# Second layer: VectorE's passes for statistics, quantisation and feed-forward at other quads of a batch

## The reference

```python
x = x + _L0_attn_ref(_layernorm(x), ...)      # layer 0: causal attention, 16 heads of 8
x = x + _L0_ffn_ref(_layernorm(x), ...)       # layer 0: 8 experts, 2 per token
x = x + _L1_attn_ref(_layernorm(x), ...)      # layer 1: full attention, 16 heads of 8
x = x + _L1_ffn_ref(_layernorm(x), ...)       # layer 1: gated, width 352

def fp4_quant_dequant(x):                     # blocks of 16 along the last axis
    scale = max(max|block| / 6, 1e-12)
    q = nearest of (0, .5, 1, 1.5, 2, 3, 4, 6) to |x / scale|
    return q * sign(x) * scale
gate, y = fp4_linear(x, w_gate), fp4_linear(x, w_up)
h = silu(gate) * y
return fp4_linear(h, w_down)                  # h is quantised too
```

## Time and profile before

| | us |
|---|---|
| median of three runs | 2297.63 (2297.55 to 2308.24) |
| profiled execution, its own time | 2295.53 |
| its span from first to last instruction | 2293.8 |
| TensorE busy | 1985.7 (87%) |
| VectorE busy | 1588.6 (69%) |
| ScalarE busy | 1396.3 (61%) |
| GpSimd busy | 1078.2 (47%) |

### The profile page before, as it was taken

The page is one execution under the profiler, slowest core; times in us unless marked ns, Lnnn a source line. Parts: engine busy times, 40 slices in busy tenths (PEclk is TensorE's granted clock), DMA queues, the critical chain, the costliest instruction groups (busy, mean ns, idle before and its releaser), DMA issues.

```text
span 2293.8 us, 45190 instructions
## 1 busy us (share of the span) xinstructions
PE 1985.7 (87%) x13603; PEld 994.7 (43%) x13603; DVE 1588.6 (69%) x4202; ACT 1396.3 (61%) x3097; POOL 1078.2 (47%) x1777
## 2 busy tenths in 40 slices
PE   2999999999999939999828889999999999899984
PEld 1455455554455419989701223333333333333333
DVE  3888888887888633332126788888888887888844
ACT  0466666666666624444305677777777777777772
POOL 6433746547455250000064565666656665664222
PEclk7899999999999969999957999999999999999997
DMA  6232223223232024444312222222222122221100
GB/s 176 79 96 68 86 75 89 76 73 92 69 92 78 24 67 144 142 136 139 108 57 72 65 62 61 65 62 61 61 65 69 57 60 65 62 61 49 54 6 14
DMA packets 167648, 174.15 MB, mean 76 GB/s; under 512 B 42544, under 2 KB 126192, under 8 KB 167280
## 3 DMA queue, kind: packets, MB, share of 16 engines
q1 hardware_dynamic: 157776, 153.87, 22.7%
q0 software_dynamic: 8192, 16.79, 2.6%
q10 hardware_dynamic: 1440, 0.60, 0.1%
HBM read 120.30 MB, written 49.28 MB: 74 GB/s over the span
## 4 chain that ended last, share of the span: by engine, by line
PE 23%; DVE 15%; issue 5%; SPq 3%; ACT 2%; POOL 2%; DMA 1%; ACTq 0%; DVEq 0%; POOLq 0%
DVE l_rowmax L1818 8%; PE bank L1604 6%; PE bank L1592 5%; PE pair L1581 3%; SPq L78 2%; PE bank L1678 2%; PE bank L1651 2%; PE pair L1658 2%; DVE l_hq L236 2%; PE bank L1618 1%; DVE l_stats L1854 1%; DVE l_hq L259 1%; POOL l_chosen_rows L1404 1%; SPq L98 1%; PE bank L1668 1%
## 5 line engine op out<-in xcount | busy, mean ns | idle before, releaser
L1818 DVE TENSOR_REDUCE l_rowmax<-pair 128x2 f32<-128x1024 f32 x512 | 597.0, 1216 | 145.7 <-PE pair L1581 145.5
L1727 ACT ACTIVATE l_probs<-bank 128x512 f32<-128x512 f32 x1024 | 554.1, 602 | 95.4 <-PE bank L1592 90.1
L907 DVE CUSTOM_DVE_ANT_0 pair<-pair,mask_rows_q 128x512 f32<-128x512 f32 (+3 forms) x1024 | 476.0, 517 | 98.3 <-PE pair L667 91.7
L823 ACT ACTIVATE l_probs<-bank 128x256 f32<-128x256 f32 (+3 forms) x769 | 307.6, 444 | 107.8 <-PE bank L679 104.6
L1592 PE MATMUL bank<-q_stack,k_stack 128*128 128x512 bf16 x1024 | 321.0, 389 | 26.2 <-DMA q_stack<-l_rowmaxT 13.6
L667 PE MATMUL pair<-k_stack,q_stack 96*128 96x512 bf16 (+3 forms) x1024 | 315.2, 313 | 25.2 <-DVE l_rowmax L907 14.9
L1604 PE MATMUL bank<-l_probs,v_aug 128*32 128x512 f32 x2048 | 276.7, 612 | 2.6 <-ACT l_oT L1772 2.6
L1581 PE MATMUL pair<-k_stack,q_stack 64*128 64x512 bf16 x1024 | 177.6, 394 | 93.3 <-DVE l_rowmax L1818 63.6
L677 PE MATMUL bank<-q_stack,k_stack 128*128 128x256 bf16 (+3 forms) x769 | 231.8, 306 | 0.2
L691 PE MATMUL bank<-l_probs,v_aug 128*32 128x512 f32 (+3 forms) x2048 | 192.2, 448 | 20.3 <-ACT l_probs L823 17.7
L1592 PEld LDWEIGHTS bank<-q_stack,k_stack 128*128 128x128 bf16 x1024 | 74.9, 97 | 253.0 <-ACT l_probs L1727 135.1
(11 more groups left out here) (286 smaller groups left out, 3383.2 us busy)
## 6 DMA issues: line engine op xcount, KB each, us to landing
q_stack<-scratch SPq DMA_DIRECT2D x192, 96.0 KB
k_stack<-scratch SPq DMA_DIRECT2D x192, 96.0 KB
experts_w<-in_w SPq DMA_DIRECT2D x72, 256.0 KB, 2.5
q_stack<-scratch SPq DMA_DIRECT2D x320, 48.0 KB
k_stack<-scratch SPq DMA_DIRECT2D x320, 48.0 KB
scratch<-l_q_parts SPq DMA_DIRECT2D x32, 384.0 KB, 2.5
scratch<-l_k_parts SPq DMA_DIRECT2D x32, 384.0 KB, 2.6
experts_rows<-rows_in SPq DMA_DIRECT2D x72, 128.0 KB, 2.2
```

Source lines behind the costliest of these rows:

```text
L823: nc.scalar.activation(probs[:, (a * HG + j) % PSLOTS, c0:S], bank[:, c0:S], ACT.Exp, scale=SCALE).then_inc(t_read, 1)
L907: nc.vector.tensor_tensor_reduce(scores, scores, m["mask_rows_q"][:, S - keys(t):S], 1.0, LOWEST, ALU.add, ALU.max, rowmax[:, g % 2, c:c + ...
L1727: nc.scalar.activation(probs[:, (a * HG + j) % PSLOTS, :], bank[:, :], ACT.Exp, scale=SCALE).then_inc(t_read, 1)
L1818: nc.vector.tensor_reduce(largest, banks[:, :].rearrange("p (k n) -> p k n", k=2), X_AXIS, ALU.max).then_inc(s_read, 1)
```

## The change

Only the tables of offsets in `layer_one` change, and with them the first and the last slot. `stats` moves from position 12 to 7, `stats4` from 0 to 15, the two `up` from one slot (position 11) into two (10 and 11) with all four `gate` in the first of them, `hquotient` from 13 to 14, `hraised` from 15 to 1, `hlowered` from 0 to 2. What depends on them moves along: `gather`, `combine` and `factors` by five slots earlier, `turn` and both `down` by one slot later.

```diff
     MIDDLE = [("rowmax", g, 4 * g + 6) for g in range(G)] + [
-        ("xnT", 0, -15), ("xqT", 0, F + 32)] + [("turn", k, F + 44) for k in range(NC)]
-    END = [("out", g, F + 4 * g + 6) for g in range(G)] + [("v", 0, 0), ("qk", 0, -9), ("qk", 1, -8)] + [("gate", t, F + 33) for t in range(2)] + [("up", 0, F + 33)] + [
-        ("gate", t, F + 33) for t in range(2, TT)] + [("up", 1, F + 33), ("down", 0, F + 45), ("down", 1, F + 53)]
-    ACT_WORK = [("normalise4", 0, F + 24), ("xsizes", 0, F + 27), ("hsizes", 0, F + 36)]
-    DVE_WORK = [("stats", 0, -20), ("stats4", 0, F + 22), ("xlargest", 0, F + 25), ("xquotient", 0, F + 26),
-                ("xraised", 0, F + 28), ("xlowered", 0, F + 29), ("hinverse", 0, F + 34), ("hquotient", 0, F + 35),
-                ("hraised", 0, F + 37), ("hlowered", 0, F + 38)]
+        ("xnT", 0, -15), ("xqT", 0, F + 31)] + [("turn", k, F + 45) for k in range(NC)]
+    END = [("out", g, F + 4 * g + 6) for g in range(G)] + [("v", 0, 0), ("qk", 0, -9), ("qk", 1, -8)]
+    END += [("gate", 0, F + 32), ("gate", 1, F + 32), ("up", 0, F + 32), ("gate", 2, F + 32), ("gate", 3, F + 32), ("up", 1, F + 33), ("down", 0, F + 46), ("down", 1, F + 54)]
+    ACT_WORK = [("normalise4", 0, F + 23), ("xsizes", 0, F + 26), ("hsizes", 0, F + 37)]
+    DVE_WORK = [("stats", 0, -25), ("stats4", 0, F + 21), ("xlargest", 0, F + 24), ("xquotient", 0, F + 25),
+                ("xraised", 0, F + 27), ("xlowered", 0, F + 28), ("hinverse", 0, F + 35), ("hquotient", 0, F + 36),
+                ("hraised", 0, F + 39), ("hlowered", 0, F + 40)]
     POOL_WORK = [("split_max", g, 4 * g + 5) for g in range(G)]
-    POOL_WORK += [("gather", k, -30 + (0, 1, 3, 4)[k // 2]) for k in range(2 * TT)]
-    POOL_WORK += [("combine", 0, -22), ("combine", 1, -21), ("factors", 0, -19), ("normalise", 0, -17),
-                  ("split", 0, -8), ("split", 1, -7), ("add_x", 0, F + 21), ("factors4", 0, F + 23),
-                  ("xscales", 0, F + 26), ("xq", 0, F + 30), ("hscales", 0, F + 34), ("hq", 0, F + 39), ("add_down", 0, F + 55)]
+    POOL_WORK += [("gather", k, -35 + (0, 1, 3, 4)[k // 2]) for k in range(2 * TT)]
+    POOL_WORK += [("combine", 0, -27), ("combine", 1, -26), ("factors", 0, -24), ("normalise", 0, -17),
+                  ("split", 0, -8), ("split", 1, -7), ("add_x", 0, F + 20), ("factors4", 0, F + 22),
+                  ("xscales", 0, F + 25), ("xq", 0, F + 29), ("hscales", 0, F + 35), ("hq", 0, F + 41), ("add_down", 0, F + 56)]
     SP_WORK = [("max_out", g, 4 * g + 7) for g in range(G)] + [("parts", 0, -6), ("parts", 1, -5)]
-    SP_WORK += [("stack", g, (-4, -2, 1, 5)[g]) for g in range(G)] + [("store", 0, F + 56)]
-    FIRST, LAST = -30, QUADS * NB + F + 41
+    SP_WORK += [("stack", g, (-4, -2, 1, 5)[g]) for g in range(G)] + [("store", 0, F + 57)]
+    FIRST, LAST = -35, QUADS * NB + F + 42
```

## The result

| | before | after |
|---|---|---|
| median of the runs, same chip | 2297.59 (2292.82 to 2308.24, 4 runs) | 2330.1 (2319.8 to 2332.07, 4 runs) |
| profiled execution, its own time | 2295.53 | 2331.56 |
| its span | 2293.8 | 2329.8 |
| first row of the layer (GpSimd's copy of the slots, L1402) | 1139.23 | 1145.21 |
| from there to the first scores | 52.73 | 64.24 |

The changed kernel is slower: ratio 1.0126, with a 95% interval from 1.008 to 1.0172. The two profiled spans differ by 36.0 us. The other 30.0 are the layer's.

A forecast was written before the change was run, and what follows sets the result against it. VectorE and TensorE take turns as the bound, so a batch costs the longer one's work per quad. Start 10.4, batches 5.6 and end 1 sum to 17 us: 2312.5 profiled, 2314.6 as median, range 2296 to 2336.

The forecast's parts named there:

- The spreading itself brings nothing: Steady batch: sum falls at positions 12, 13, 15 and rises at 1, 2, 8, 10; plus 0.5 us a batch.
- the longer list: Per position, the longer of VectorE's and TensorE's own work; sums to 63.6 us a batch before, 64.1 after.
- the fourth rival: Spreading works: TensorE's wait for VectorE falls from 4.0 to 1.0 us a batch, 42 saved, 2267 in total; chance 0.08.
- The stall behind the table load: Position 11: TensorE stands 1.2 us for ScalarE's exponential, the later last up no longer covering the load; plus 1.0 a batch.
- the drain rival: ScalarE's table switch: an uncovered drain as long as the load, 1.28 us, and the collision staying; 30 more, 2344; chance 0.08.
- Position 11: Place of the table load's standstill of 1.2 us, forecast to rise from VectorE's 3.99 to 5.0.
- the 0.8 a batch: Handovers the plain sum lacks: of 1.1 us a batch, 0.8 kept because the stall behind normalise4 falls under position 2.
- `hquotient`'s collision goes: Position 14: GpSimd's normalise ends before hquotient starts, taking 0.84 us off each batch; bounds 0.84 and nothing.
- The first rival: Collision stays: GpSimd is 0.9 late, hquotient keeps its 2.45 us; 14 x 0.84 = 12 more, 2326; chance 0.12.
- The start: GpSimd's queue before quad 0: batch 1's combine and factors precede batch 0's split, first scores 10.4 us later; bounds 10 and 12.
- the third rival: The start is paid back: quad slack absorbs the table stall and more, 0.7 to 0.8 us a batch; 2298; chance 0.22.
- The end: Last batch: stats4 moves earlier while hlowered and what follows fall later; plus 1 us, between -3 and +2.

The follow-up runs named there:

- e7: Kernel before with only turn, down, hq, add_down, store and the passes on h at their new offsets: 2302.28 us (1 run), batch 65.5 to 66.5.
- e4: Kernel before with stats, gather, combine and factors five slots earlier for batches 2 and up: 2290.44 us (1 run), batch 64.28.
- e8: Kernel before with stats, gather, combine and factors five slots earlier from batch 2, hlowered one slot later: 2277.57 us (4 runs), ratio 0.9915.
- e5: Changed kernel with a plain copy of the gate in place of silu, so no table switch: 2316.49 us (1 run), batch 65.92.
- e6: Kernel before with a plain copy of the gate in place of silu, so no table switch: 2291.3 us (1 run), batch 64.69.
- e3: Changed kernel with add_down, and store with it, two slots later on GpSimd: 2317.18 us (1 run), batch 65.65.
- e10: Changed kernel with normalise five slots earlier and add_down eight later: 2353.31 us (1 run, kernel before 2360.93 there), batch 65.27.
- e1: Changed kernel with batches 0 and 1 keeping the old offsets of gather, combine, factors and stats: 2322.88 us (1 run).
- the reordered one: Kernel before with stats and GpSimd's entries moved from batch 2, hlowered one slot later: 2311.33 us, ratio 0.9788; again 2325.73 us, ratio 0.9811.
- e11: Kernel before, unchanged, run again in a group where its median was 2371.4 us: 2372.59 us (1 run), batch 66.3 to 69.5.

## Why the prediction came out right, and what in it was wrong

Forecast was 2314.6 within 2296 to 2336, and slower at 0.62; measured 2330.1. The direction and most of the mechanisms held, but a steady batch grew by 1.53, four times the 0.4 that I gave it and more than my upper bound of 1.3. That the batches together stayed under the +18 of that bound is luck: only seven of the 13 intervals grew by the full 1.5. Held against the account above, the sum of 17 was 2.2 short at the start, 10.1 short in the batches (15.7 for 5.6) and 0.8 short at the end; with them it makes the layer's 30.

- **The spreading itself brings nothing** (+0.5 a batch): the positions agree where neither a collision nor the split `up` reaches (0, 4 and 12 are 0.3 to 0.4 shorter than the longer list, the others within 0.1), but no run shows the 0.5 alone. TensorE's waits for the maxima fell by 1.3 a batch, short of the 3 that the fourth rival wanted, and the new neighbours took more than that. The parts run apart have opposite signs: the passes on `h` alone cost 0.9 to 1.8 (e7, with a collision that the change doesn't have), the statistics alone gain 0.4 (e4), the statistics with `hlowered` alone gain 1.3 (e8). For e7 the same two lists had forecast -0.7 to +0.4, so there they missed the sign.
- **The stall behind the table load** (1.2, place and sign): held, 1.17 once a batch, and 1.41 at its position when the switch was taken away (e5). That before it was covered held too (e6). No drain beside the load showed: the first exponential starts 0.01 behind the load's end, in agreement with the earlier trace rows and against the estimate of 2.6 from the Trainium skill ("ScalarE: Activation LUTs", What ACT_TABLE_LOAD costs). So the drain rival fell. What I had not seen is that taking the stall away only moves VectorE into another collision.
- **Position 11** was forecast at 5.0 with the stall and measured 6.44; without the load it is 5.03 (e5), not 3.99. The rest is the handover of the second `up`, for which VectorE waits 0.94 in e5 and 2.36 with the load. So position 11 is 1.44 over the forecast. In the sum that is hidden by two things, the 0.8 a batch that I had kept for handovers and positions 0, 4 and 12, which came out 0.96 shorter together than forecast. Without this luck the batch would have been missed by more.
- **`hquotient`'s collision goes**: held, 1.62. **The step that was mis-sized stands right behind it.** I worked out GpSimd's arrival for the one collision that the trace of before showed, and for none of those that the new order could make. There were three: `hraised` with `add_down` (0.55, e3), the divisor of `hinverse` with `normalise` (0.36, e10) and `xraised` with `combine` (0.3 by the rows alone, as no run removed it: position 5 takes 3.17 in place of 2.87). The first two are 0.93 of the 1.1 a batch by which 66.2 lies above my 65.1. With them out of the way, e10 has 65.27. The first rival (the collision stays, 14 x 0.84, 2326) came near the price, 0.93, at the wrong place. The rule of the Trainium skill ("SBUF — State Buffer", SBUF: two separate sides) agrees with the rows of `hraised` and of e4's `xquotient`: both have two inputs in SBUF, meet a pass of GpSimd that reads SBUF, and end about one undisturbed duration behind it (1.49 for 1.61, and 0.54 for 0.69). I should have put it to every pass that the diff moves.
- **The start** (+10.4, bounds 10 to 12): held, 10.25 at `split`, 11.5 at the first scores, and 10.5 undone by e1. With the first `hquotient` 1.1 later by its own position, nothing of it is given back by then, and the batches after it cost more, not less. So the third rival, that the start is paid back, fell.
- **The end** (+1, bounds -3 to +2): 4.0 by the stretch behind the last maxima, outside the bounds (1.8 in the account above). But the kernel before itself shows 94.5 and 92.8 in two runs, and the reordered one 91.9 and 97.0, so less than some 5 us of it can't be told from chance by single traces.
- The median came out 32.5 above before's, and 6.0 of the profiled difference of 36.0 lie ahead of the layer, for which I had no term.

## What to carry to other kernels

When a queue that is ordered by hand is reordered, walk through the other engine's queue once for each pass that moves, and also for each small pass in front of it: which long SBUF pass of GpSimd runs at its new place? Two lists of busy times, quad by quad, gave the right sign for the whole change and most of the places, but the wrong sign for e7: a pass that fits beside TensorE can still double by a neighbour that the lists don't have. Don't split a product away from work that covers something else (here a table load); and move the offsets of the first two iterations separately, since nothing covers them.

## What the runs showed of the hardware

- A pass of VectorE with one small input is also held up by GpSimd: 128 x 32 floats took 1.86 beside a pass of `hq` (e7), and 128 x 88 took 1.71 beside `add_x` and `normalise` (e5), where they take 0.18 and 0.20 alone. The rows of these two end 0.04 and 0.08 behind GpSimd's, so their duration is nearly all waiting.
- It works in both directions. In the kernel before, GpSimd's copy of 128 x 16, 0.20 alone, took 1.52 and ended 0.05 behind VectorE's `hraised` (1490.28, 1.61 long):

```profile
1490.42 1.52 POOL L1473 CAST l_rowmax_parts<-l_rowmax 128x16 bf16<-128x16 f32 x1 [2.47 <-DVE l_rowmax L1818]
```

- A held-up pass pulls all that is behind it on its queue: TensorE's 1.78 in e7 comes from a pass that has 0.2 us of work.
- The same kernel can differ by more than this change from one group of runs to another: the kernel before took 2294.5 to 2297.6 in some and 2360.9 to 2371.4 in others. Of the spans, 37 to 48 us of it lie ahead of the layer (first row at 1139 or at 1176 to 1187), and in e11, the only trace of it with the longer time, a batch is 1.6 to 4.9 us longer, mostly at positions 4 and 6. Not every order shows it: e10 ran in such a group too, and its positions are those of the changed kernel on the first chips within 0.02, apart from the two that its edit shortened. Why is open.
